# Attention and feed-forward part in one program, with float16 pairs in all products and the feed-forward weights split in pairs 9 to 14

## The reference

```python
q, k, v = (einsum('bsd,dhk->bshk', resid, W) for W in (W_Q, W_K, W_V))
scores = where(causal_mask, MASK_FILL, einsum('bqhc,bshc->bhqs', q, k) / sqrt(64))
z = einsum('bhqs,bshc->bqhc', softmax(scores), v)
x = layernorm(resid + einsum('bqhc,chd->bqd', z, W_out) + b_out)
h = (x - mean(x)) * rsqrt(var(x) + EPS) * ln_gamma + ln_beta
w1, w2 = (q - 128) * scales        # fc1: 256 x 1024, fc2: 1024 x 256, scales by groups of 128 rows
y = silu(h @ w1 + fc1_bias)
out = layernorm(x + x + 0.5 * (y @ w2 + fc2_bias))
```

## Time and profile before

| | |
|---|---|
| median of three runs | 1804.33 us (1804.23 to 1804.38) |
| the profiled execution, own time | 1803.28 us |
| its span, first to last instruction | 1801.5 us |
| mean granted TensorE clock | 0.987 |
| busy: TensorE, weight loads | 1703.7 us (95%), 1209.2 us (67%) |
| busy: VectorE, ScalarE, GpSimd | 1374.6 (76%), 1503.7 (83%), 1357.2 us (75%) |
| granted clock from 1540 to 1780 us (middle blocks) | 1.00 (2.4 GHz) |

### The profile page before, as it was taken

One profiled execution on the slowest core, in us unless ns is written; L12 is line 12 of the kernel. 1 busy time (PEld: TensorE's weight loads), 2 busy tenths in 40 slices (PEclk: granted clock), 3 DMA queues, 4 the chain that ended last, 5 costly groups with the idle time before them and its releaser, 6 DMA issues. The chain is left out here.

```text
span 1801.5 us, 53858 instructions
## 1 busy us (share of the span) xinstructions
PE 1703.7 (95%) x21836; PEld 1209.2 (67%) x21836; DVE 1374.6 (76%) x3164; ACT 1503.7 (83%) x3165; POOL 1357.2 (75%) x826
## 2 busy tenths in 40 slices
PE   4799999999999999999999999999999985899997
PEld 2466666666666666666666666666666654789886
DVE  7979797878787778888889787979787844656553
ACT  4599999999999999999999999999999981465464
POOL 3498989898989897989888989898988890332232
PEclk9899999999999999999999999999999998999999
DMA  4013121202020202121212121111111209222200
GB/s 134 13 23 98 21 52 17 57 16 57 14 60 12 56 17 57 20 78 20 57 20 57 20 54 24 50 26 49 25 49 25 49 14 340 77 74 71 94 13 24
DMA packets 113207, 91.82 MB, mean 51 GB/s; under 512 B 73152, under 2 KB 100032, under 8 KB 111808
## 3 DMA queue, kind: packets, MB, share of 16 engines
q1 hardware_dynamic: 112960, 88.38, 18.2%
HBM read 33.82 MB, written 20.97 MB: 30 GB/s over the span
## 5 line engine op out<-in xcount | busy, mean ns | idle before, releaser
L459 POOL TENSOR_TENSOR p_lo<-p_full,p_hi 128x1024 f16<-128x1024 f32 (+1 forms) x640 | 1161.1, 1841 | 215.4 <-ACT p_full L556 212.8
L555 ACT ACTIVATE p_hi<-psum 128x512 f16<-128x512 f32 (+3 forms) x1280 | 718.7, 562 | 71.5 <-PE psum L854 42.6
L556 ACT ACTIVATE p_full<-psum 128x512 f32<-128x512 f32 (+3 forms) x1280 | 724.8, 569 | 0.0
L612 DVE TENSOR_REDUCE row_max<-psum 128x1 f32<-128x512 f32 x768 | 485.8, 682 | 30.8 <-PE psum L820 27.1
L876 PE MATMUL psum<-v,p_hi 128*128 128x65 f16 x4352 | 487.5, 193 | 5.9 <-POOL p_lo L459 3.9
L878 PE MATMUL psum<-v,p_hi 128*128 128x64 f16 x4352 | 488.9, 194 | 0.0
L880 PE MATMUL psum<-v,p_lo 128*128 128x65 f16 x4352 | 486.5, 192 | 0.0
L876 PEld LDWEIGHTS psum<-v,p_hi 128*128 128x128 f16 x4352 | 407.2, 97 | 81.5 <-POOL p_lo L459 11.5
L850 PE MATMUL psum<-qa,ka 128*128 128x512 f16 (+3 forms) x1280 | 444.4, 348 | 15.8 <-ACT p_full L556 14.8
L878 PEld LDWEIGHTS psum<-v,p_hi 128*128 128x128 f16 x4352 | 403.2, 97 | 70.9 <-issue 0.8
L854 PE MATMUL psum<-qb,kb 128*128 128x512 f16 (+3 forms) x1280 | 444.1, 348 | 1.5 <-DVE qb L625 1.4
(11 more groups left out here) (127 smaller groups left out, 2669.2 us busy)
## 6 DMA issues: line engine op xcount, KB each, us to landing
zT_dram<-z_T SPq DMA_DIRECT2D x16, 1024.0 KB, 4.2
z_rest<-zT_dram SPq DMA_DIRECT2D x5, 2048.0 KB, 10.3
qb<-qa SPq DMA_DIRECT2D x128, 64.0 KB, 1.9
ka<-ka SPq DMA_DIRECT2D x128, 64.0 KB, 1.9
shared_z<-zT_dram SPq DMA_DIRECT2D x3, 2048.0 KB, 9.8
shared_z<-xT_dram SPq DMA_DIRECT2D x8, 512.0 KB, 7.1
xs<-x_dram SPq DMA_DIRECT2D x8, 512.0 KB, 10.5
out_dram<-res SPq DMA_DIRECT2D x8, 512.0 KB, 3.2
```

The lines of the kernel that those rows point to most:

```text
L459: nc.gpsimd.tensor_tensor(p_lo[:, at % NP, cols], p_full[:, at % NP, cols], p_hi[:, at % NP, cols], ALU.subtract).then_inc(probs_split, 1)
L555: nc.scalar.activation(p_hi[:, at % NP, to], lane_bank(a)[:, P * f:QB], ACT.Exp, scale=1.0 / SCORE)
L556: nc.scalar.activation(p_full[:, at % NP, to], lane_bank(a)[:, P * f:QB], ACT.Exp, scale=1.0 / SCORE).then_inc(lane_read, 1)
L612: nc.vector.reduce_max(most, bank, AX.X).then_inc(ring_read, 1)
```

## The change

1. One program with one block: each engine runs its attention list and then its feed-forward list. The feed-forward tensors lie in attention's memory (x_hi, x_lo, w_hi, q, k, p).
2. fc1 and fc2 take float16 pairs. Scales (powers of two from bounds on gamma, beta, bias and the weights) are made on the chip, in a `scales` step with 15 small VectorE instructions. Per F tile ScalarE does Silu (with scale `u_inverse`), a scaled Copy to a_hi and a scaled Copy in place.
3. The feed-forward weights are loaded in unit 8 (15 DMAs), dequantised in 8 pieces in units 9 to 12 (`ffn_full`), and split in 8 pieces in units 13 and 14 (`ffn_parts`).
4. z of blocks 0 and 1, x of both and the biases are loaded at the start of unit 15 (`load_ffn`), which waits for the last group's products. z has two buffers instead of three.
5. Out projection 1 sums in the ZO banks; out projection 2 moves from the end of step 0 ahead of it.
6. Side steps of attention get other slots.

```diff
-Z_BUFS = 3
+Z_BUFS = 2
-W_STEPS = [12, 22, 32]
-X_PEAK_UNIT, X_PEAK_STEPS, X_SPLIT_UNIT, X_SPLIT_STEPS = 1, [8, 22], 3, [12, 24]
-WO_PEAK_UNIT, WO_PEAK_STEPS, WO_SPLIT_UNIT, WO_SPLIT_STEPS = 8, [10, 24], 10, [10, 26]
-CHAIN_STEPS = [30, 32]
+W_STEPS = [11, 30, 38]
+X_PEAK_UNIT, X_PEAK_STEPS, X_SPLIT_UNIT, X_SPLIT_STEPS = 1, [24, 26], 3, [21, 37]
+WO_PEAK_UNIT, WO_PEAK_STEPS, WO_SPLIT_UNIT, WO_SPLIT_STEPS = 8, [24, 26], 10, [10, 29]
+CHAIN_STEPS = [32, 33]
+W_PIECES, FULL_UNIT, FULL_STEPS, PART_UNIT, PART_STEPS = 4, 9, [24, 32], 13, [11, 21, 30, 37]
+FFN_CHAIN = [33, 34]
...
+            def load_ffn_weights():
...
+                sp.dma_start(gam[:, :], gamma).then_inc(q_in[0], 16)
...
+                for w, (q, scales) in enumerate(((q1, s1), (q2, s2))):
+                    k, n = scales.shape
+                    sp.dma_start(w_full[w].bitcast(I32).rearrange("p (k n) -> p k n", k=k), q.rearrange("(k p) n -> p k n", p=P)
+                                 ).then_inc(q_in[w], 16)
+                    for r in range(k):
+                        sp.dma_start(w_scales[w][:, n * r:n * r + n], scales[r:r + 1, :].to_broadcast([P, n])).then_inc(q_in[w], 16)
+            def load_ffn():
+                sp.wait_ge(wo_split, PAIRS)
...
+                sp.dma_start(z_bufs[0].rearrange("p g a t -> p g (a t)"), zT_dram[0].rearrange("p g a t -> p g (a t)")
+                             ).then_inc(early_in, 16)
+                for at in [("group", UNITS - 1, GROUPS - 1), ("values", UNITS - 1, NQ - 1)]:
+                    sp.wait_ge(ring_ready, RING_AT[at] + 1)
+                    sp.sem_inc(passed, 1)
+                sp.wait_ge(w_halved, W_PIECES)
...
+            def split_ffn(j):
...
+                act.wait_ge(scaled, 5)
+                nc.scalar.activation(w_halves[w][0][:, cols], w_full[w][:, cols], ACT.Copy, scale=s).then_inc(w_high, 1)
+                act.wait_ge(w_high, j + 1)
+                nc.scalar.activation(w_full[w][:, cols], w_full[w][:, cols], ACT.Copy, scale=s).then_inc(w_scaled, 1)
...
+            def ffn_full(m, j):
...
+                nc.vector.scalar_tensor_tensor(out=w_full[w][:, cols], in0=w_full[w][:, cols].bitcast(I32), scalar=-128.0,
+                                               in1=w_scales[w][:, cols], op0=ALU.add, op1=ALU.mult).then_inc(w_dequantised, 1)
+                dve.wait_ge(w_dequantised, j + 1)
+                nc.vector.tensor_reduce(w_piece[:, j:j + 1], w_full[w][:, cols], axis=AX.X, op=ALU.max,
+                                        apply_absolute_value=True).then_inc(peaked, 1)
...
-                if more == 2:
+                if more == 2 and i:
                     out_projection(i + 2)
 
             pe.wait_ge(wo_split, PAIRS)
             pe.wait_ge(early_in, 16)
+            pe.wait_ge(lane_read, len(LANE_AT))
             out_projection(0)
+            pe.wait_ge(ring_read, len(RING_AT))
+            pe.wait_ge(z_done, UNITS * NBLK)
             out_projection(1)
             turn(0)
-            pe.wait_ge(w1_split, W_STEPS)
+            out_projection(2)
+            pe.wait_ge(w_halved, 2 * W_PIECES)
             over_blocks(pe, step)
...
-                    for dst in (a_hi[:, f, :], a_full[:, f % 2, :]):
-                        last = nc.scalar.activation(dst, psum[:, FC + f % 2, :], ACT.Silu, bias=b1_s[:, f:f + 1])
-                    last.then_inc(act_ready, 1)
+                    at = i * FT + f + 1
+                    nc.scalar.activation(a_full[:, f % 2, :], psum[:, FC + f % 2, :], ACT.Silu, bias=b1_s[:, f:f + 1],
+                                         scale=u_inverse[:, :]).then_inc(silu_done, 1)
+                    act.wait_ge(silu_done, at)
+                    nc.scalar.activation(a_hi[:, f, :], a_full[:, f % 2, :], ACT.Copy, scale=a_scale[:, :]).then_inc(a_high, 1)
+                    act.wait_ge(a_high, at)
+                    nc.scalar.activation(a_full[:, f % 2, :], a_full[:, f % 2, :], ACT.Copy,
+                                         scale=a_scale[:, :]).then_inc(act_ready, 1)
```

More of the change, by code:

```diff
@@ L240, in peaks_before, with program @@
     seen = ORDER[:ORDER.index(at)]
-    return sum((x[0] in ("w_peak", "x_peak", "wo_peak")) + (x[0] == "x_peak" and x[3] == NQ - 1) for x in seen)
+    return sum((x[0] in ("w_peak", "x_peak", "wo_peak", "ffn_full")) + (x[0] == "x_peak" and x[3] == NQ - 1)
+               + (x[0] == "ffn_full" and x[2] % W_PIECES == W_PIECES - 1) + 3 * (x[0] == "ffn_full" and x[2] == 0) for x in seen)
 def lane_place(m, i, u):
     return LANE_AT[("scores", m, i, u)]
-def attention(nc, shared, ident, z_T, z_stored, z_power, early_in, wo_split, xT, wqkv, zT_dram, wout):
+def program(nc, x, xT, wqkv, wout, b_out, gamma, beta, q1, s1, b1, q2, s2, b2, out, zT_dram):
     with ExitStack() as ctx:
@@ L322, in attention @@
         wo_loaded, wo_hi_done = sem("wo_loaded"), sem("wo_hi_done")
-        block = ctx.enter_context(nc.Block())
+        z_stored, early_in, wo_split = sem("z_stored"), sem("early_in"), sem("wo_split")
+        q_in, biases_in = [sem("q1_in"), sem("q2_in")], sem("biases_in")
+        z_in, x_in = [sem(f"z_in{k}") for k in range(Z_BUFS)], [sem("x_in0"), sem("x_in1")]
+        w_dequantised, w_high, w_scaled, w_halved, b2_halved = (sem(n) for n in ("w_dequantised", "w_high", "w_scaled", "w_halved", "b2_halved"))
+        wo_ready, wo_read = sem("wo_ready"), sem("wo_read")
+        first_norms, last_norm = sem("first_norms"), sem("last_norm")
+        norm_ready, hT_ps, hT_parts, hT_ready = sem("norm_ready"), sem("hT_ps"), sem("hT_parts"), sem("hT_ready")
+        var_ready, std_ready = sem("var_ready"), sem("std_ready")
+        fc1_ready, act_ready, a_split = sem("fc1_ready"), sem("act_ready"), sem("a_split")
+        fc2_used = sem("fc2_used")
+        fc2_read = sem("fc2_read")
+        res_ready = sem("res_ready")
+        preloaded = sem("preloaded")
+        silu_done, a_high = sem("silu_done"), sem("a_high")
+        stored = [sem("stored0"), sem("stored1")]
+        x_blk = x.rearrange("b (q t p) d -> (b q) p t d", t=TPB, p=P)
+        out_blk = out.rearrange("b (q t p) d -> (b q) p t d", t=TPB, p=P)
+        MLAG = 3
+        W_COLS = DF // W_PIECES
         SHIFT_ROWS = 6
@@ L574, in _ @@
                     split_x(*x)
+                if what == "ffn_parts":
+                    split_ffn(*x)
                 if what == "x_part":
@@ L757, in _ @@
                     outputs(m, *x)
+                if what == "ffn_full":
+                    ffn_full(m, *x)
                 if what == "wo_peak":
@@ L1252, in _ @@
+            nc.vector.tensor_scalar(hb2, b2_s, 0.5, None, ALU.mult).then_inc(b2_halved, 1)
+            dve.wait_ge(b2_halved, 1)
             to_norms(0, 0, 0)
-            dve.wait_ge(q2_in, 16 * (1 + FT))
-            dequantise(Chain(w2_split, 1), q2s, s2s)
             to_hT(0)
             over_blocks(dve, step)
+        block = ctx.enter_context(nc.Block())
+        @block.sync
+        def _(sp):
+            attention_sync(sp)
+            feed_forward_sync(sp)
+        @block.gpsimd
+        def _(pool):
+            attention_gpsimd(pool)
+            feed_forward_gpsimd(pool)
@@ L1276 @@
+    program(nc, x, xT, wqkv, wout, b_out, gamma, beta, q1, s1, b1, q2, s2, b2, out, zT_dram)
 def kernel(**inputs):
```

303 lines of the change are left out of this document (164 added, 139 removed).

## The result

| | before | changed |
|---|---|---|
| median (lowest to highest, 7 runs each) | 1804.33 us (1800.42 to 1808.6) | 1813.47 us (1811.29 to 1815.43) |
| span of the profiled execution | 1801.5 us | 1811.4 us |
| attention's last product ends | 1486.1 us | 1483.3 us |
| from there to the end | 315.4 us | 328.1 us |

The ratio is 1.005, 95% interval 1.0039 to 1.0061: slower by half a per cent, where I had predicted 1799.5 us, 0.27% faster. Attention gained 2.8 us (predicted 4.7) and all behind it lost 12.7 (predicted 0.6).

What follows compares the result with a forecast made beforehand. TensorE bounds attention and the middle blocks now; ScalarE was to bound the changed blocks. Terms +0.6 -14.3 +4.3 +1.5 +3.3 +0.5 = -4.1 us gave about 1800, stated as 1799.5 us; range 1788 to 1812.

Steps and rivals of the forecast that it cites:

- The transition: From attention to feed-forward: out projection 0 can start at 1486.1, block 0's first product at 1518.6 instead of 1535.9 us.
- ScalarE as the new bound of the blocks: Feed-forward blocks: three ScalarE activations take 2.19 us per F tile; a middle block takes 38.05 us, 3.9 more than before.
- rival 1: Feed-forward loop: TensorE stays the bound, 6 us less for each of seven blocks, about 1758 us; chance 0.06.
- The last tile's low part: End of each feed-forward block: the low part of the last activation tile takes about 1.25 us, against 1.30 before.
- 5.3 to block 7's Silu and 20.2 for its eight tiles: Last block: 5.3 us from block 6's end to its Silu, then 20.2 for eight tiles without roots, ending at 1793.5.
- Rival 4: Feed-forward loop: stalls drop the clock to 1.2 GHz, 14 us more per block, 1890 us if in most; chance 0.04.
- The chain of small VectorE steps at 33, 34 of unit 12: Attention unit 12, small VectorE steps at slots 33 and 34: costs +1.5 us, bounds 0 and 3.
- The slots: Attention units 0 to 6: moving weight and x side steps into ScalarE's gaps saves 14.3 us, bounds 5 and 19.
- SyncE's queue: Loads queued ahead of copies that attention needs: +3.3 us in unit 15 (bounds 0 and 8), +0.5 in unit 8 (0 and 6).
- the splits: Units 13 and 14: eight feed-forward weight splits on ScalarE, with W_out's part beside one, cost +4.3 us, bounds 1 and 12.

Runs made afterwards that it cites:

- two-Silu run: Changed kernel with two Silu reads per F tile on float16 pairs instead of one Silu and two Copies, activations unscaled: 1767.85 us.
- filler's run: Changed kernel with the products of the second fc1 tile done four times over in blocks 1 and 7: 1809.7 us.
- one-column run: Changed kernel with three operations of unit 12's scale chain (a_bound, gam_s, bet_s) as tensor_scalars on one column each: 1807.09 us.

## Why the prediction was wrong

Two steps of the sum failed, and both left out the same thing, that VectorE and GpSimd can make each other wait: the chain in unit 12 was put at +1.5 and cost 8.6, and the last low part of a block was put at 1.25 us and took 2.20. The rest of the miss behind attention is the clock, which the sum had at nothing, and a tile price that doesn't hold in block 7.

**The transition: right.** The first out projection started 0.4 us behind attention's last product, and block 0's first product 33 us after it (predicted 32.5).

**ScalarE as the new bound of the blocks: right.** 2.19 us a tile, 2.81 for a root with its loads, products that wait for ScalarE (1.09 us at the third tile). The two-Silu run shows that rival 1, TensorE staying the bound, is what this change would have needed.

**"The last tile's low part (about 1.25; now 1.30)": wrong.** I took it for the same operation as before. In the changed block it falls together with hT_lo and takes 2.20. With that undone a middle block is 37.98 us, where the prediction had 38.05. The term was 1.04 us short in each of seven blocks, 7.3 in all. (The closeness of 38.05 is in part a slip: the terms as written, 17.6, twice 2.9, 1.55, 1.25 and 1.3, add to 27.5 and not to 27.65, which makes a block 37.9 and the forecast about 1 us lower.)

**"5.3 to block 7's Silu and 20.2 for its eight tiles": wrong by 3.4.** The 5.3 came out (last product 1773.8, Silu 1779.07), the tiles took 23.5. Of that 1.9 is the clock, by the filler's run, in this execution (0.5 to 2.6 by the others without a filler). Rival 4 had named the wait and priced a fall that holds for whole blocks; it held for the twelve products behind it. The other 1.4 was there with the filler too (21.6 us for the tiles): in the second half of a block with no root TensorE itself is the bound, with 2.61 us for each pair of fc1 and fc2, and my sum had ScalarE's 2.19 for each tile. Block 1 took 33.5 us from last product to last product (predicted 31.5): 1.0 collision and 1.1 clock.

Behind attention that is 7.3, 1.9, 1.1 and 1.4, or 11.7 of the 12.1 us missed.

**"The chain of small VectorE steps at 33, 34 of unit 12: +1.5, bounds 0 and 3": the largest single miss.** It was +8.6. Taking the chain out gave 7.4 us. Of these 2.9 are the operations' waits for GpSimd and some 2.7 the clock behind the resulting wait of TensorE, since the one-column run gave 5.6 in unit 12 for 2.9 in the chain (an estimate from the table of stretches agrees: four microseconds at 0.50 and four at 0.79 lose 2.0 and 0.8); 1.9 are the operations at their own length, near the 1.5 predicted. The bound of 3 took each operation at its own length. The other 1.2 of the 8.6 stayed in unit 12 without the chain, and what they are wasn't tried. Unit 9, which has a like chain for W_out, came out 2.1 us longer (predicted 0), with 1.98 us for a product of two 128x8 tensors beside GpSimd; putting that in single columns gave 0.66 back, and what the rest is wasn't tried.

**The slots: right.** Units 1 to 6 together are 15.0 us shorter, predicted 12.5, and 2.0 of that was unit 5 of the execution before, which the slots don't explain. Units 13 and 14 cost 2.9, predicted 4.3.

**"SyncE's queue: +3.3 and +0.5": wrong by 4.** Units 8 and 15 are no longer than before. I had all of unit 15's loads begin with the copies at 1419; they are issued from 1409.1 on, and the copies behind them, issued by 1424.3, landed by 1431.7, in time for the chunk that needs them. A rate of 2 MB in 10.3 us for one load at a time was too low as well: the six loads and the store overlapped, each 7.8 to 10.4 us from issue to landing.

Together: attention missed by +1.9 (the chain +7.1, unit 9 to 11 +1.5, start and unit 0 +1.4, against the slots -2.5, the splits -1.4 and the queue -4.1), the rest by +12.1: 14.0 us, from -4.1 to +9.9. That attention as a whole missed by so little is luck: +10 and -8 stand against each other. Start and unit 0 say nothing, since unit 0 lasted 107.2 to 112.2 us in the executions of all these kernels.

## What to carry to other kernels

Before a chain of small VectorE operations is placed, look at what GpSimd does in that moment: here forms with two tensor inputs, and tensor_scalars over two or eight columns, lasted at least until its instruction under way ended, while one-column tensor_scalars passed. Price a longer wait of TensorE with what follows it (here waits of 3.2 and 4.9 us were followed by 1 to 2.7 us lost at the lower clock); and count what a merged or reordered block brings side by side that was apart before. Where one engine is near the bound, as ScalarE was, one more activation in the loop can cost more than all else saves: here the third activation and its wait on 64 F tiles cost 46 us.
